# One head in four without second scores: its probabilities as a product of two exponentials, multiplied by Pool, and the values between the third and fourth scores

## What is computed

```python
feats   = einsum('bnf,hfo->bhno', h, kernel)                 # values, 16 per head
f_self  = einsum('bnf,hfd->hbnd', h, attention_kernel)
f_other = einsum('bnf,hfd->hbdn', h, attention_kernel_2)
scores  = einsum('hbnd,hbdm->hbnm', f_self, f_other)         # 1500 x 1500 per batch and head
masked  = a_h * scores
masked  = where(masked >= 0, masked, 0.2 * masked) / 4
masked  = masked + where(a_h == 0, -1e9, 0)
attn    = softmax(masked, axis=-1) * where(a_h == 0, 0, 1)
out     = layernorm(x + relu(einsum('bhnm,bhmo->bhno', attn, feats) + bias))
```

## Time and profile before

| | |
|---|---|
| time, median of 3 runs | 928.04 us (927.79 to 928.58) |
| the profiled execution | 928.04 us, its span 926.2 us |
| mean granted TensorE clock | 0.973 of full |
| busy: PE, DVE, ACT, Pool | 868.7, 785.4, 630.3, 299.8 us |

### The profile page before, as it was taken

One profiled execution on the slowest core, in us unless ns is written; L12 is line 12 of the kernel. 1 busy time (PEld: TensorE's weight loads), 2 busy tenths in 40 slices (PEclk: granted clock), 3 DMA queues, 4 the chain that ended last, 5 costly groups with the idle time before them and its releaser, 6 DMA issues.

```text
span 926.2 us, 14045 instructions
## 1 busy us (share of the span) xinstructions
PE 868.7 (94%) x4956; PEld 279.7 (30%) x4956; DVE 785.4 (85%) x1509; ACT 630.3 (68%) x1244; POOL 299.8 (32%) x280
## 2 busy tenths in 40 slices
PE   4089999999999999999999999999999999999994
PEld 3022332233233233333322332332333333222231
DVE  3168889988999989898899889999899988999994
ACT  2057776777677776777767776777767777677773
POOL 5042081233543063330921335430633309202101
PEclk7579999999999999999999999999999999999998
DMA  9795479853895849926797538947599258974000
GB/s 240 128 259 135 154 122 239 204 154 81 123 277 145 197 86 185 294 59 156 121 258 203 124 107 133 299 117 198 85 202 278 62 153 127 255 182 64 18 1 17
DMA packets 198396, 144.53 MB, mean 156 GB/s; under 512 B 177104, under 2 KB 177104, under 8 KB 198320
## 3 DMA queue, kind: packets, MB, share of 16 engines
q1 hardware_dynamic: 195152, 139.91, 64.5%
q10 hardware_dynamic: 3168, 3.67, 2.4%
HBM read 94.08 MB, written 12.51 MB: 115 GB/s over the span
## 4 chain that ended last, share of the span: by engine, by line
PE 88%; issue 4%; DVE 2%; DMA 2%; SPq 2%; POOL 1%; ACT 0%; POOLq 0%; DVEq 0%
PE z L495 54%; PE numer L519 29%; PE misc L428 2%; DVE z L785 1%; PE misc L470 1%; SPq L220 1%; DMA edges<-in_adj 1%; PE misc L434 1%; DMA x_sb<-in_x 1%; POOL mask L323 1%; PE misc L421 1%; DVE norm L721 0%; DMA maskT<-mask 0%; DVE ob L807 0%; SPq L212 0%
## 5 line engine op out<-in xcount | busy, mean ns | idle before, releaser
L785 DVE SCALAR_TENSOR_TENSOR z<-z,maskT 128x512 f32<-128x512 f32 (+1 forms) x1152 | 725.4, 680 | 111.7 <-PE z L495 105.0
L690 ACT ACTIVATE probs<-z 128x512 f32<-128x512 f32 (+1 forms) x1152 | 596.9, 593 | 257.9 <-PE z L495 257.9
L495 PE MATMUL z<-self_st,other_st 96*128 96x512 bf16 (+3 forms) x2304 | 561.2, 378 | 25.0 <-issue 24.7
L495 PEld LDWEIGHTS z<-self_st,other_st 96*128 96x128 bf16 (+1 forms) x2304 | 189.6, 98 | 477.0 <-ACT probs L690 306.7
L519 PE MATMUL numer<-probs,vals 128*32 128x512 f32 (+1 forms) x2304 | 301.1, 595 | 0.2 <-ACT probs L690 0.2
L323 POOL TENSOR_SCALAR mask<-edges 128x1500 int16<-128x1500 f32 x96 | 138.3, 1441 | 93.2 <-DMA maskT<-mask 44.7
L368 POOL TENSOR_TENSOR cent<-yb,mean 128x256 f32<-128x256 f32 x24 | 14.7, 612 | 299.0 <-DVE mean L820 299.0
L352 POOL TENSOR_SCALAR part<-proj 128x512 bf16<-128x512 f32 x21 | 12.5, 618 | 218.7 <-ACT proj L625 218.7
L519 PEld LDWEIGHTS numer<-probs,vals 128*32 128x32 f32 x2304 | 45.3, 108 | 118.2 <-ACT probs L690 95.6
L359 POOL TENSOR_TENSOR part<-rest,part 128x512 bf16<-128x512 f32 x21 | 23.7, 1157 | 0.0
L354 POOL TENSOR_TENSOR rest<-proj,part 128x512 f32<-128x512 f32 x21 | 23.7, 1157 | 0.0
(11 more groups left out here) (67 smaller groups left out, 210.0 us busy)
## 6 DMA issues: line engine op xcount, KB each, us to landing
edges<-in_adj SPq DMA_DIRECT2D x88, 750.0 KB, 6.0
parts_dram<-part SPq DMA_DIRECT2D x21, 384.0 KB, 5.6
self_st<-parts_dram SPq DMA_DIRECT2D x42, 192.0 KB, 5.9
other_st<-parts_dram SPq DMA_DIRECT2D x42, 192.0 KB, 6.3
edges<-in_adj SPq DMA_DIRECT2D x8, 468.8 KB
x_sb<-in_x SPq DMA_DIRECT2D x8, 352.0 KB
out<-cent SPq DMA_DIRECT2D x8, 352.0 KB
maskT<-mask SPq DMA_TRANSPOSE x96, 6.4
```

Of the source, the lines that this page charges most:

```text
L495: return nc.tensor.matmul(z[:, v % BUFS * STEP + i, 0:WIDTH[st]], other_st[par][rows, h, c * P:(c + 1) * P], self_st[par][rows, h, st * W: ...
L690: nc.scalar.activation(probs[:, g % PROBS, v % UNITS * STEP:(v % UNITS + 1) * STEP, 0:WIDTH[st]], z[:, v % BUFS * STEP:(v % BUFS + 1) * ST ...
L785: nc.vector.scalar_tensor_tensor(banks, banks, FLOOR, maskT[(par + st) % 2][:, c, 0:WIDTH[st]].unsqueeze(1).broadcast_to([P, STEP, WIDTH[s ...
```

## The change

Head 0 of each group (`LEAK = 0`) loses its lift. VectorE writes its masked part into its slot of `probs` in SBUF, and the bank keeps the plain scores. ScalarE takes two exponentials, of the bank into a new buffer `lows` and of the slot in place, and Pool multiplies the slot by `lows`. The values wait for Pool as well (`pooled`). `ORDER` has no lift of a fourth head, and the values stand ahead of the fourth score. Lifts are counted over three heads (`LIFTS`), with a lag of 3 lifts.

So that Pool can come to a product in every group, its blocks are spread over the groups by tables (`MASKS_AT`, `SPLITS_AT`, `SHIFT_AT`, `SCALE_AT`, `CENTER_AT`). The squares move from Pool to ScalarE. Three prep rounds move forward. The path for large scores (not taken here) becomes a second copy of the body of PE and DVE at the end of their programs.

```diff
-ORDER = (("s", 0), ("l", 0), ("s", 1), ("l", 1), ("s", 2), ("l", 2), ("s", 3), ("l", 3), ("v", 0))
-PREP_AT = [36, 40, 74, 78, 82, 86, 90, 120, 124]
+ORDER = (("s", 0), ("l", 0), ("s", 1), ("l", 1), ("s", 2), ("l", 2), ("v", 0), ("s", 3))
+PREP_AT = [36, 40, 44, 48, 52, 76, 80, 120, 124]
+PREP_LAG = 3
 OUT_AT = 13
 NUMER_AT = 4
-FINISH_AT = (None, 16, 19, 22, 25, 28, 31, 34, 45)
-ROOT_AT = 46
+FINISH_AT = (None, 16, 19, 22, 25, 28, 31, 34, 46)
+ROOT_AT = 47
+MASKS_AT = ({0: 0, 1: 1, 2: 2, 3: 3}, {0: 0, 1: 1, 2: 2, 3: 3}, {3: 0, 4: 1, 5: 2, 6: 3})
+SPLITS_AT = ({}, {4: (0, 1), 5: (2,), 6: (3,), 7: (4,), 8: (5,), 10: (6, 7), 11: (8,)}, {0: (9,), 1: (10,), 2: (11,)})
+SHIFT_AT = 5
+SCALE_AT = 7
+CENTER_AT = 9
...
+            def multiply(g, b, par):
+
+                st = g // NT
+                p = probs[:, g % PROBS, LEAK, 0:WIDTH[st]]
+                pool.wait_ge(grown, at(b, GB, g + 1))
+                pool.tensor_tensor(p, p, lows[:, g % 2, 0:WIDTH[st]], ALU.mult).then_inc(pooled, 1)
...
+                    for c in range(NT):
+                        multiply(st * NT + c, b, par)
+                        if c in MASKS_AT[st] and not (last and st == NS - 1):
+                            make_mask(b, st + 1, MASKS_AT[st][c])
+                        if c in SPLITS_AT[st] and not last:
...
             def values(g, b, par):
                 st, c = g // NT, g % NT
                 pe.wait_ge(expd, at(b, VB, UNITS * (g + 1) + BUFS))
+                pe.wait_ge(pooled, at(b, GB, g + 1))
...
-                    m = take_proj(proj, misc, r - XT_ROUNDS)
+                    p = r - XT_ROUNDS
+                    take_proj(proj, misc, p)
+                    m = nc.scalar.activation(squares[:, p * W:(p + 1) * W], misc[:, 0:W], ACT.Square)
...
+                    if v % UNITS == LEAK:
+                        act.wait_ge(raised, at(b, GB, g + 1))
+                        if b or g >= 2:
+
+                            act.wait_ge(pooled, at(b, GB, g - 1))
+                        nc.scalar.activation(lows[:, g % 2, 0:WIDTH[st]], bank, ACT.Exp, scale=LOW).then_inc(expd, 1)
+                        nc.scalar.activation(slot, slot, ACT.Exp, scale=LOW).then_inc(grown, 1)
+                    else:
+                        if v % UNITS == 1:
+
+                            act.wait_ge(pv_done, at(b, GB, g + 1))
+                        act.wait_ge(lifted, at(b, LB, g * LIFTS + v % UNITS))
+                        nc.scalar.activation(slot, bank, ACT.Exp, scale=LOW).then_inc(expd, 1)
...
+                dve.wait_ge(pv_done, at(b, GB, g + 1))
+                if not large:
+                    masked_part(slot, v, par).then_inc(raised, 1)
```

More of the change, by code:

```diff
@@ L159, in gat_layer @@
         lifted = sem("lifted")
+        raised = sem("raised")
         expd = sem("expd")
+        grown = sem("grown")
+        pooled = sem("pooled")
         pv_done = sem("pv_done")
@@ L180, in gat_layer @@
         big_scored = sem("big_scored")
+        big_lifted = [sem(f"big_lifted{p}") for p in range(2)]
+        big_masked = sem("big_masked")
         big_read = sem("big_read")
@@ L379, in batch @@
                 for st in range(NS):
[L380 to L394, removed]
-                    elif st == 1:
-                        if not last:
-                            pool.wait_ge(parts_out, at(b, 48, 48))
-                            for k in range(SPLITS):
+                    for c in range(NT):
[3 more added lines that the diff above has]
+                        if c in SPLITS_AT[st] and not last:
+                            for k in SPLITS_AT[st][c]:
@@ L409, in batch @@
+                        if c == SCALE_AT and st == NS - 1 and not first:
                             scale_rows(b - 1, 1 - par)
-                        center(b, par, 1)
+                        if c == CENTER_AT and not (first and st == 0):
+                            center(b, par, st - 1)
             batches(batch)
@@ L598, in _ @@
             out_round(use(B - 1, NS + 1))
+            pe.br("pe_done")
+            batches(large_batch)
+            nc.switch_bb("pe_done")
         @block.scalar
@@ L868, in _, with units @@
             dve.wait_ge(bias_in, 16)
-            def batch(b, par, first=False, last=False):
-                dve.wait_ge(safe_ready, at(b, 1, 1))
-                small = dve.value_load(safe[par][0:1, 0:1], min_val=0, max_val=1)
-                with dve.If(small == 0):
+            def units(b, par, first, last, large):
+                if large:
                     large_scores(b)
-                with dve.Else():
+                else:
                     dve.sem_inc(big_read, MAXIMA)
@@ L889, in batch, with large_batch @@
                         inverse_root((v - ROOT_AT) // ROOT_EVERY, b - 1)
+            starts = []
+            def batch(b, par, first=False, last=False):
+                dve.wait_ge(safe_ready, at(b, 1, 1))
+                small = dve.value_load(safe[par][0:1, 0:1], min_val=0, max_val=1)
+                starts.append(nc.cur_bb)
+                dve.br_ne(small, 1, on_true=f"dve_large{b}", on_false=f"dve_small{b}")
+                nc.switch_bb(f"dve_small{b}")
+                units(b, par, first, last, large=False)
+                dve.br(f"dve_next{b}")
+                nc.switch_bb(f"dve_next{b}", parent=starts[b])
+            def large_batch(b, par, first=False, last=False):
+                with nc.body(f"dve_large{b}", parent=starts[b], valid_engines=[mybir.EngineType.DVE]):
+                    units(b, par, first, last, large=True)
+                    dve.br(f"dve_next{b}")
             batches(batch)
```

150 lines of the change are left out of this document (88 added, 62 removed).

## The result

The changed kernel takes 949.22 us (median of 4 runs, 947.27 to 954.47) beside 928.31 for the kernel before: ratio 1.0234, 95% interval 1.019 to 1.0277. It is slower; whether by more than 2%, the interval leaves open. The profiled execution took 947.27 us, 19.2 more than the profiled one before.

What follows compares the result with a forecast made beforehand. PE's own row of products was taken to set the pace, with DVE, ACT and Pool close below. 928.0 - 61.7 + 18 (root steps) + 12 (epilogue) + 7 (norms) + 3 (x) = 906 us; 80% range 876 to 938.

Steps and rivals of the forecast that it cites:

- removed products: On PE, one lift fewer in each group: 7.7 us a batch, 61.7 us in 8 batches; plain group 2.85 to 2.63.
- root steps behind the product: Stage 1: DVE's two-input inverse-root steps wait for Pool's product, nine a batch at 0.37 us, less 0.8; +18 us.
- a wait for x or `numer_free`: Wait for the load of x or of the values for `numer_free`: 0.4 us a batch, +3 us (0 to 10).
- norms round: PE's wait for DVE's reduction before round two at unit 124 grows by the values' 0.95 us: 7 batches, +7 us.
- squares and ACT: Three squares a batch moved to ACT, counted in ACT's 92 us a batch, below PE's 100.3; no added cost.
- epilogue: Epilogue's two-input DVE steps wait for Pool at groups 6 and 7: 0.5, 0.5, 1.0 us over the stages; +12 (0 to 25).
- the rival on the slower side: Root steps wait nearly a full product, perhaps single-input ones too; kernel 938, or 920 to 945; chance 0.2 in all.
- the third rival: ACT becomes the bound: SBUF exponential 0.60 us, or takes with squares in three groups running; 920 us, chance 0.1.
- PE keeps the pace: Rival: root steps slip past Pool's product; only the norms wait and a little epilogue stay; 878 us, chance 0.2.
- The waits eat the gain: Rival: 15 two-input DVE steps a batch each wait 0.93 us for Pool; kernel 938 us, chance 0.2 in all.
- the signs I had named: Plain groups 2.63 us, root steps 0.5 to 0.7, stages 0, 1, 2 at 34.2, 37.5, 33.8, norms idle 1.4 or more.

Runs made afterwards that it cites:

- both memsets: Two runs, each against the changed kernel: the twelve inverse-root steps replaced by memsets, 914.6 us; Pool's product replaced by a memset, 914.94 us.
- x a group later: Changed kernel with the first five prep rounds, which read the load of x, 4 units later: 929.24 us.
- edges behind x: Changed kernel with stage 0's edge loads issued behind the load of x and not between the transposes: 929.63 us.
- product as a memset: Changed kernel with Pool's product replaced by a memset of the same slot, all waits kept: 914.94 us.
- no squares: Changed kernel without ACT's later squares; the norms test reads those of the first batch: 950.22 us.
- The kernel with the norms round later: Changed kernel with the second norms round at unit 128 and not 124: 940.49 us.
- moving it by one tile: Changed kernel with root steps one unit earlier, behind the third mask of a group and not the fourth: 934.73 us, ratio 1.0041 to the kernel before.
- three moves in its tables: Changed kernel with root steps at 46, first five prep rounds 4 units later, second norms round at 128: 902.24 us, ratio 0.9715 to the kernel before.

## Why the prediction was wrong

The sum was 906, in a range of 876 to 938; 949 lies outside it. The root's mechanism was right and its size too small; the load of x was named and not priced; the squares, the norms test's L780 and the clock had no cost in the sum. By the terms of the sum:

| term | forecast | measured | by |
|---|---|---|---|
| removed products | -61.7 | plain group 2.63 for 2.85 | trace of after |
| root steps behind the product | +18 | +27 | both memsets, stage 1 |
| a wait for x or `numer_free` | +3 | 18 to 20 | x a group later, edges behind x |
| norms round | +7 | wait 0.52 to 1.14 a batch, +4.3 | traces of before and after |
| norms test's L780 | 0 | 0.77 for 0.15, 0.5 a stage 2 | product as a memset |
| squares and ACT | 0 | +7, in its stage | no squares |
| epilogue | +12 (its parts give 14) | DVE 5.5 busier in it; what the stages lose not known | traces of before and after |

**The step that failed most** is the last of the sum, "a wait there, or of the values for `numer_free`, I put at 0.4 us a batch". I had put its two causes side by side (x nearer to the other transfers, its reader sooner in time) and priced neither. Pool's masks, once a block and now one to a group, put the last edge load 17.5 us into the stage (11.7 before), 2.2 us ahead of x. Transfers at work beside others took 5.3 to 6.9 us to land in the earlier trace rows, and the reader left x 4.4: up to 2.5 us a batch, 17 in seven, was to be had from rows that I had chosen myself, and the upper end that I wrote was 10. That the cause is the crowding is shown by moving the edges alone. PE's own wait is 11.6 us of the 18 to 20; the clock behind it, at its lower level for 10.2 us in the middle batches, is a further part, and I had no term for it.

**The root term** was mis-sized, and its rule held: a step that met the product ended with it, and in the last batch the period was 3.12 us for 3.0. In a middle batch I had nine steps at 0.37 us, less 0.8. It was six steps, five at the product and one at a split, at 0.3 to 1.1 us over their own 0.16, 4.1 in all. Two numbers were low. The product takes 1.27 us, and not 1.04: I took the row with the right inputs and a bf16 output (L357), and the one with the f32 output (L354, 1.11 to 1.16), nearer, is still too low. And where the splits make the product late, the step meets it at its start, 1.25 us for a forecast 0.6. In the last batch the three single-input steps wait as well, 0.81 to 1.13 us for 0.16; that was in the rival on the slower side and not in the sum.

The Trainium skill ("SBUF — State Buffer", Who interferes with whom) says that `tensor_scalar` can enter a mode that takes the shared port, that two-input operations contend with GpSimd's reads but not with one that only writes, and that the loser blocks for the whole instruction. The trace agrees: 0.81 us for the single-input L894 beside a product, and 0.44 beside a memset, which only writes; 0.16 for two-input steps inside memsets; and ends that coincide within 0.03 us. Which mode L894 ran in no run shows. I had quoted the first and given it a chance of at most 0.2 because no row showed it.

**The squares** cost a stage 1 us because three groups with a projection have seven ACT instructions, and ACT was part of their bound. I had this as the third rival ("takes of 1 us with squares come in three groups running") and not in the sum. An SBUF exponential takes 0.65 us and one from PSUM 0.62, but the next instruction starts 0.50 and 0.52 us behind theirs (864.91, 865.41, then a copy at 865.93 in the last batch), so that half of the rival fell.

**A term I had not seen** is in the first batch: two memsets on Pool, 2.65 us each, ahead of a product, with PE 2.46 us behind them. The clock makes it dearer: from 77.35 on it was at its lower level for 6.83 us, and the stage took 39.70 us. The kernel with the norms round later has the same wait and no fall, and takes 36.19; before, it was 36.14. So most of what the first batch lost is the clock.

```profile
71.45 2.65 POOL L391 MEMSET other_st<- 3x3072 f32 x1
...
75.59 1.07 PE L542 MATMUL numer<-probs,vals 128*32 128x512 f32 x8 [2.46 <-POOL probs L381]
```

**The rivals.** "PE keeps the pace" fell as a whole: in the middle batches the first steps did come past the product, behind the long groups of the projections, and the last six did not. "The waits eat the gain" came nearest; its mechanism is shown, but its 938 lacked x. Of the signs I had named, the plain group came, and the root steps in part (forecast 0.5 to 0.7 us, measured 0.16 to 1.25); stage 1 came at 40.4 and not 37.5, stage 0 at 36.3 and not 34.2, stage 2 at 34.3 and not 33.8, and PE's wait ahead of the norms transpose at 1.14 us and not 1.4.

**What stays open.** The single effects, 27 + 19 + 7 + 7 + 2.5 for the memsets, make 62 us of the 81 that the kernel lost against 928 - 61.7 = 866. That is an upper figure, since the kernel before had 0.52 us a batch of the norms' wait too. For the rest, some 18 or more, no run shows a cause; I had put 12 on the epilogues. In stage 2 it is 1.4 us a batch (33.28 with the norms wait gone, 31.9 by the products alone). Why the clock falls in some batches and not in others, with waits as near as 1.66 and 1.83 us, was not tried either.

## What to carry to other kernels

When work moves to Pool, list every small DVE operation that runs beside it, those with one input too, and price each at what is left of the Pool instruction that it can meet, and not at its own time. That is a matter of phase: moving it by one tile gave back two thirds of what removing it did (here 2.5 of 3.7 us a stage). When a block on one engine is spread out, follow the transfers that it releases: they spread as well, and the next load in that queue shares its time with them. A wait of TensorE can cost more than its length, so read the granted clock of the stretch behind it, and compare single effects by stage: here waits and clock in stage 0 took back 5.5 us of one gain and hid another. Undo suspects one by one before giving up a change: this one was 2% slower as it came and 3% faster with three moves in its tables.

## What the runs showed of the hardware

- A 12-element DVE operation from SBUF to SBUF takes 0.16 us alone and ends 0.01 to 0.03 us behind the end of a Pool instruction that reads SBUF: 0.81 us beside a product, 1.04 beside a split, 1.40 beside a mask of 1500 elements (L898). Single-input `tensor_scalar`, int32 (L894, L898) and f32 (L892, 1.13 us), is no exception.
- Beside a Pool memset (0.52 us, write only) a two-input operation takes 0.16 us and can end before the memset does. A single-input `tensor_scalar` is held by it too: 0.44 us for 0.16, ending 0.03 us behind it.
- Behind waits of PE of 1.66 to 2.65 us for x the granted clock was at 1.2 GHz for 3.41 us in three batches of six; in the others it stayed at 2.4 GHz.
- Pool's product of two f32 tiles into f32, in place, takes 1.27 us for 128x512 and 1.20 for 476 columns; the product of a 128x512 f32 tile with itself into bf16 took 1.04.
- A load issued 2.2 us behind the last edge load had not landed after 5.5 us; with the edge loads behind it, it was there within 3.7.
